# Graph stage of a four-layer graph network: logits built on ScalarE, shifted before the transpose, exponentiated on the way out of PSUM

## What is computed

```python
h = jnp.einsum('bnd,ade->bane', feat_in, W)
th = jnp.tanh(h)
attn_src = jnp.einsum('bane,aeo->bano', th, w_src)
attn_dst = jnp.einsum('bane,aeo->bano', th, w_dst)
attn = attn_src + jnp.swapaxes(attn_dst, 2, 3)
attn = jnp.where(attn >= 0, attn, LEAKY_ALPHA * attn)        # 0.2
attn = jnp.where(mask, jnp.float32(-999.0), attn)
attn = jax.nn.softmax(attn, axis=-1)
feat_out = jnp.einsum('banm,bame->bane', attn, h) + b
...
feat_out = jax.nn.elu(feat_out)
gate = jax.nn.sigmoid(feat_in @ H_w.T + H_b)
return gate * feat_out + (1.0 - gate) * feat_in
```

## Time and profile before

| | us |
|---|---|
| median of three runs | 2711.53 |
| the profiled execution | 2709.26 |
| its span | 2707.5 |
| busy in the span: TensorE, VectorE, ScalarE, GpSimd | 2640.9, 2417.2, 2346.9, 1804.9 |

### The profile page before, as it was taken

One profiled execution on the slowest core, in us unless ns is written; L12 is line 12 of the kernel. 1 busy time (PEld: TensorE's weight loads), 2 busy tenths in 40 slices (PEclk: granted clock), 3 DMA queues, 4 the chain that ended last, 5 costly groups with the idle time before them and its releaser, 6 DMA issues. The chain is left out here.

```text
span 2707.5 us, 66704 instructions
## 1 busy us (share of the span) xinstructions
PE 2640.9 (98%) x20128; PEld 2385.9 (88%) x20128; DVE 2417.2 (89%) x7209; ACT 2346.9 (87%) x6600; POOL 1804.9 (67%) x1550
## 2 busy tenths in 40 slices
PE   8999999999998999999999999999999999999996
PEld 7888888888887999999999999899999999999995
DVE  6998998898887999999999999899999999999995
ACT  7999999999998888888888888888888888888884
POOL 3777766766765677766666677766666666667665
PEclk9999999999999999999999999999999999999998
DMA  3011111111104888887778888878778887878775
GB/s 99 28 38 40 33 34 39 33 33 39 37 29 130 256 260 259 263 253 252 247 252 255 256 262 264 252 255 251 253 242 259 256 250 254 253 245 257 250 249 176
DMA packets 386754, 500.42 MB, mean 185 GB/s; under 512 B 58464, under 2 KB 349152, under 8 KB 386272
## 3 DMA queue, kind: packets, MB, share of 16 engines
q1 hardware_dynamic: 386400, 496.16, 58.2%
HBM read 219.24 MB, written 201.33 MB: 155 GB/s over the span
## 5 line engine op out<-in xcount | busy, mean ns | idle before, releaser
L794 ACT ACTIVATE probs<-logits,nmax 128x256 f32<-128x256 f32 x1152 | 571.8, 500 | 104.5 <-DVE turned_sb L1072 99.6
L570 POOL TENSOR_TENSOR probs<-probs,recs 128x1024 f32<-128x1024 f32 x288 | 545.9, 1896 | 107.8 <-DVE recs L1064 107.6
L1072 DVE STREAM_TRANSPOSE turned_sb<-probs 128x512 f32<-128x512 f32 x576 | 610.7, 1103 | 4.0 <-POOL probs L570 4.0
L1051 DVE CUSTOM_DVE_ANT_0 logits<-s,mask 128x256 f32<-128x256 f32 x1152 | 430.8, 420 | 84.1 <-PE s L1456 81.4
L548 POOL TENSOR_TENSOR residual<-x,br 128x384 f32<-128x384 f32 x192 | 191.0, 1017 | 455.9 <-DVE mix L1083 455.8
L787 ACT ACTIVATE stack<-split 64x768 fp32r<-64x768 f32 x576 | 484.8, 842 | 3.4
L76 PE MATMUL pj<-xt_hi,w_lo 128*128 128x256 f32 x1728 | 481.9, 279 | 0.8 <-DVE xt_lo L1036 0.8
L78 PE MATMUL pj<-xt_hi,w_hi 128*128 128x256 f32 x1728 | 481.0, 278 | 0.0
L77 PE MATMUL pj<-xt_lo,w_hi 128*128 128x256 f32 x1728 | 480.8, 278 | 0.0
L665 ACT ACTIVATE g_exps<-g_v,g_nmax 128x256 f32<-128x256 f32 x768 | 385.3, 515 | 3.0 <-DVE g_nmax L961 0.7
L779 ACT ACTIVATE split<-pj,bc 128x256 fp32r<-128x256 f32 x576 | 239.6, 467 | 163.2 <-PE pj L78 107.3
(11 more groups left out here) (118 smaller groups left out, 7401.3 us busy)
## 6 DMA issues: line engine op xcount, KB each, us to landing
turned<-turned_sb SPq DMA_DIRECT2D x288, 512.0 KB, 5.0
pt_copy<-turned SPq DMA_DIRECT2D x288, 512.0 KB, 4.6
stack<-split SPq DMA_DIRECT2D x576, 128.0 KB, 4.4
y<-out SPq DMA_DIRECT2D x128, 384.0 KB, 5.2
x<-y SPq DMA_DIRECT2D x96, 384.0 KB, 3.1
x<-x SPq DMA_DIRECT2D x32, 384.0 KB, 3.0
adj<-adj SPq DMA_DIRECT2D x128, 64.0 KB, 3.1
w_whole<-att_w SPq DMA_DIRECT2D x24, 192.0 KB, 2.9
```

The costliest lines, as they stand in the source:

```text
L570: pool.tensor_tensor(probs[:, heads, :, :].rearrange("p h t n -> p (h t) n"), probs[:, heads, :, :].rearrange("p h t n -> p (h t) n"), rec ...
L794: last = act.activation(probs[:, (HEADS * u + h) % 4, t, :], logits[:, h % 2, t, :], ACT.Exp, scale=-1.0, bias=nmax[:, u, h, t:t + 1], acc ...
L1051: last = dve.tensor_tensor_reduce(out=logits[:, h % 2, t, :], in0=s_ps[h % 2][:, t, :], in1=mask[u][:, t, :], scale=-HEAD_DIM ** -0.5, sca ...
L1072: last = dve.transpose(turned_sb[b][:, :, :].rearrange("p k (z h q) -> p k z h q", z=NT, h=2 * NT)[:, :, kt], probs[:, 2 * b:2 * b + 2, :, ...
```

## The change

The graph stage is written anew; the attention stage's functions stay (its first samples' order within `crossing()` is rewritten, and one store moves). The pieces:

```diff
+            def g_high_x(half, u, t):        # ScalarE; was the copy in g_lo_of_step on VectorE
+                act.activation(xt_hi[:, :, t * P:(t + 1) * P], pj_ps[g_X_BANK[t]][:, 0:D]..., ACT.Identity).then_inc(g_xt_hi_done, 1)
...
-                act.activation(g_v_sb[:, h % 3], s_ps[h % 2][:, :, :], ACT.Relu, scale=-0.8).then_inc(g_lrelu, 1)
+            def g_leaky(half, u, h):
+                g_targets_ready(act, half, u, h)
+                for t in range(NT):
+                    last = act.activation(g_v_of(u, h)[:, t, :], g_targets[u][:, h, :], ACT.Prelu, scale=-1.0,
+                                          bias=g_source[u][:, t, h:h + 1], alpha=LEAKY)
...
-                for t in range(NT):
-                    last = act.activation(g_exps[:, h % 4, t, :], g_v_sb[:, h % 3, t, :], ACT.Exp, scale=-1.0,
-                                          bias=g_nmax[:, u, h, t:t + 1], accum_out=g_sums[:, u, h, t:t + 1])
+                act.activation(g_pt_sb[:, g_pt_slot(u, h)], pt_ps[h % 2][:, :, :], ACT.Exp, scale=-1.0).then_inc(g_exped, 1)
...
                     last = dve.tensor_tensor_reduce(
-                        out=g_v_sb[:, h % 3, t, :], in0=s_ps[h % 2][:, t, :], in1=g_v_sb[:, h % 3, t, :], scale=-1.0,
+                        out=v[:, t, :], in0=s_ps[0][:, t, :], in1=v[:, t, :], scale=-1.0,
...
+            def g_subtract(half, u, h):      # VectorE, even heads
+                for t in range(NT):
+                    last = dve.scalar_tensor_tensor(v[:, t, :], v[:, t, :], g_nmax[:, u, h, t:t + 1], s_ps[0][:, t, :], ALU.subtract, ALU.max)
...
+            def g_subtract(half, u, h):      # GpSimd, odd heads
+                pool.tensor_tensor(v, v, g_nmax[:, u, h, :].unsqueeze(2).to_broadcast([P, NT, N]), ALU.subtract).then_inc(g_odd_shifted, 1)
...
-                pe.matmul(s_ps[h % 2][:, :, :], g_ident_r[:, :], g_mask[u][:, :, :], start=True, stop=False)
-                for t in range(NT):
-                    last = pe.matmul(s_ps[h % 2][:, t, :], g_z_left[u][:, t * P:(t + 1) * P], g_z_right[u][:, h, :], start=False, stop=t == NT - 1)
+                pe.matmul(s_ps[0][:, :, :], g_ident_r[:, :], g_mask[u][:, :, :], start=True, stop=True).then_inc(g_mask_laid, 1)
...
+                        pe.matmul(s_ps[1][i * GAT_DIM:(i + 1) * GAT_DIM, 0, :], ones, g_pt_sb[:, g_pt_slot(u, g * g_QUAD + i), kt, :], ...
...
+                    last = pe.matmul(pj_ps[g_SD_BANK][:, 0:N], g_sd[:, c, :], g_tt[:, c, :], start=c == 0, stop=c == DC - 1)
...
+                sp.dma_start(targets_dram[u], g_rows[g_TARGETS, :]).then_inc(g_rows_laid, 16)
+                sp.dma_start(g_targets[u][:, heads, :], targets_dram[u, heads, :]....partition_broadcast(P)...).then_inc(g_targets_spread[u][i], 16)
```

More of the change, by code:

```diff
@@ L19 @@
 GAT_HEADS, GAT_DIM = 12, 32
+LEAKY = 0.2
 HEADS, HEAD_DIM = 6, 64
@@ L41, in f32, with g_every_slot, sample @@
     return ap.bitcast(F32)
[L44 to L50, removed]
+def g_every_slot(slot):
+    def sample(k):
+        return divmod(k, 2) if 0 <= k < B else None
+    for k in range(B):
+        slot(sample(k + 1), sample(k), sample(k - 1), sample(k - 2), sample(k - 3), sample(k - 4))
 def every_slot_of_all_layers(slot, behind=3):
@@ new lines, in g_gate_tanh, with g_slot @@
+                act.activation(g_gate[u][:, t, :], pj_ps[g_GATE_BANK[t]][:, 0:D], ACT.Tanh, scale=0.5).then_inc(g_gate_done, 1)
+            def g_slot(far, nxt, cur, prev, old, done):
+                if prev:
+                    g_exp(*prev, 7)
+                    g_leaky(*prev, 11)
+                if old:
+                    g_elu_exp(*old)
+                if nxt and nxt != first:
+                    g_high_x(*nxt, 0)
+                if prev:
+                    g_exp(*prev, 8)
+                    g_copy_ct(*prev, 1)
+                    g_exp(*prev, 9)
+                if cur:
+                    g_leaky(*cur, 0)
+                    g_leaky(*cur, 1)
+                    g_gate_tanh(*cur, 0)
+                if prev:
+                    g_exp(*prev, 10)
+                if cur:
@@ L1268, in g_make_back @@
-            def g_make_back(half, u, t, cur, nxt):
+                pe.matmul(out, g_ones[:, :], g_hb[:, :], start=False, stop=True).then_inc(g_gate_made, 1)
+            def g_make_back(half, u, t):
+                if half == HALVES - 1:
+                    if (half, u, t) == (*g_even, 0):
+                        pe.wait_ge(g_gate_done, at(NT, *g_odd, NT))
+                    pe.wait_ge(g_back_read, at(NT, half, u, t))
+                elif t == 0:
+                    pe.wait_ge(g_tt_ready, at(NT, half, u, 2 * NT + 1))
+                else:
+                    pe.wait_ge(g_tt_ready, at(NT, half, u, 3 * NT))
@@ L1269, in g_make_back @@
                 if t == 0:
                     pe.wait_ge(g_ctx_read, at(g_GROUPS, half, u, g_GROUPS))
[L1271 to L1276 removed]
+                    pe.wait_ge(g_sums_read, at(1, half, u, 1))
@@ L1301, in g_four_contexts, with g_sums_of_four @@
+            def g_sums_of_four(u, g):
+                ones = g_sel[:, 1 + g * GAT_DIM:1 + (g + 1) * GAT_DIM]
+                for kt in range(NT):
+                    for i in range(g_QUAD):
+                        pe.matmul(s_ps[1][i * GAT_DIM:(i + 1) * GAT_DIM, 0, :], ones, g_pt_sb[:, g_pt_slot(u, g * g_QUAD + i), kt, :],
+                                         start=g == 0 and kt == 0, stop=g == g_GROUPS - 1 and kt == NT - 1)
             def g_four_contexts(half, u, g):
                 first = g * g_QUAD
-                pe.wait_ge(g_pt_even_read, g_evictions(half, u, first + g_QUAD - 2))
```

923 lines of the change are left out of this document (456 added, 467 removed).

## The result

| | before | changed |
|---|---|---|
| median | 2711.7 | 2643.6 |
| lowest and highest of 4 | 2705.3 to 2715.6 | 2642.3 to 2644.8 |
| profiled execution | 2709.26 | 2642.26 |
| its span | 2707.5 | 2640.5 |

The ratio is 0.9751, with a 95% interval of 0.9731 to 0.9771: 68 us faster. 2640 was predicted, within 2602 to 2685.

The account below looks back on a forecast made before the run. The bound was to move from ScalarE and TensorE to TensorE alone at 22.2 us, period 22.8. From 2709.3, minus 75 for 31 periods, plus 5 for the ends, gives 2639, stated as 2640 us, range 2602 to 2685.

Parts of the forecast that it names:

- The four sums: Graph stage, busy us per sample of each engine after the change: TensorE 22.2, VectorE 21.1, ScalarE 20.8, GpSimd 17.96.
- the leaky step: ScalarE's new leaky half, from one start to the next: taken as 0.40 us, within 0.36 to 0.50.
- the sources and targets: TensorE's three added full-width fp32 matmuls: at most 0.5 us each, taken as 1.5 us a sample.
- The period: Graph stage, time per sample: 22.8 us, 2.42 less than before, times 31 periods 75 us saved.
- the ends: First leaky half waits for two landings, +4 us; last sample drags four more heads into the crossing, +1.
- The bound: Graph stage: moves from ScalarE and TensorE at 24.9 and 24.7 us to TensorE alone at 22.2.
- three handoffs: TensorE's waits behind the state's turning and the exponentials of heads 3 and 7: 0.1 us each added.
- The sign named for it: Profile of the graph stage: TensorE's busy share highest, ScalarE and VectorE near 21 us a sample.
- The hold: VectorE standing behind GpSimd, up to 1.04 us each; one leaves TensorE the bound, two give 2661, three 2695; chance 0.15.
- The late transfer: Next sample's first spreading transfer on SP's list: 10.4 us until its leaky half needs it, landing 4.6 or 15.7.
- The rival of 2805: Spreading transfer lands in 15.7 us, too late for the leaky half; period 28.1, about 2805 us; chance 0.05.
- The copy of x: x's high part moved from VectorE to ScalarE: two copies, 0.8 us a sample added on ScalarE.

## Why the prediction was right, and where it was not

**The four sums.** ScalarE 20.8 predicted, 21.2 measured, with the leaky step at 0.40 as taken; what the other 0.4 is was not sought. VectorE 21.1 predicted, 21.6 measured: of this, 0.72 is the held gate product, so the list itself is 20.9. TensorE 22.2 predicted, 22.3 measured, or 22.0 without what a wait adds to the last matmul ahead of it. The sums at 0.89 instead of 1.00 a group and the sources and targets at 1.33 instead of 1.5 take off 0.5. A term that was put at nothing gives 0.3 back: with the scores matmuls gone, the groups of nine matmuls of 384 columns stand behind transposes or contexts in all four places, and their first one steps 0.26 to 0.28 (302.94, 305.82, 310.23 and 319.76); before, it stepped 0.17 in three places, behind scores matmuls, and 0.27 in the fourth, behind transposes. Together that is the 22.0. GpSimd 17.96 predicted, 18.7 measured, since one subtraction in each sample takes 1.69 in place of 1.04.

**The period.** 22.8 predicted, 22.89 measured, 31 times 2.33 is 72. The runs gained 68, the profiled executions 67, which leaves the +5 that was taken for the ends. The size held; that it did so with the bound named wrong is in part luck, as the next paragraph shows.

**The bound.** That the bound moves "to TensorE alone at 22.2" failed. TensorE's 0.60 of waiting matched the 0.65 allowed for (0.35 kept from before and 0.3 for three handoffs), but only 0.20 of it was a place named, the turning of the state. The contexts after heads 3 and 7 cost TensorE nothing that shows. The other 0.43 was the low part of x, which came late because VectorE was late. The step that failed is the comparison of busy sums alone: waits were added to TensorE's sum and none to VectorE's. VectorE has 1.30 of them, 0.49 behind the sums turned back and 0.57 behind leaky halves among them. (That 21.6 + 1.3 is as much as 22.3 + 0.6 proves nothing, since busy and idle time add up to the period on every engine.) The experiments show it both ways, 1.6 us off TensorE for nothing and 0.4 off VectorE for about 10 us. That TensorE's figure of 22.8 came out right was luck: it followed VectorE, and with VectorE out of the way the same matmuls went at 22.23 and, without the last wait, 22.08. The sign named for it, TensorE's busy share the highest, came true at 97.4% and could not tell.

**The hold.** The place was named (L986 against head 11's subtraction) and one hold was priced at up to 1.04 and called harmless. It was 0.72, and not harmless: taking it away at the price of a later head 11 gained 9 us, and halving it by an order that also hands TensorE its operand earlier gained 21. The forecast that VectorE's subtractions would stay out of the conflict because their second tensor is in PSUM held, and is worth more than the whole change: 97 us are lost with the other operand.

**The late transfer.** 10.4 us of room were estimated, 8.1 are there, and 5.5 are used. The rival of 2805 needed a landing of 15.7 us, scaled by size from one that was seen at the start; the same bytes landed in 5.5, so that scaling was wrong. Ahead of need there are 2.6 us and more, and a transfer issued 3.9 us ahead of its use costs 27 us.

**The copy of x.** Costed at 0.8 on ScalarE for a little more off VectorE's list; the trade is +22 us before and -21 us in the changed kernel.

## What to carry to other kernels

A busy share does not tell which engine sets the pace: one at 94% with a few short waits did here, and one at 97% followed it. Busy time plus idle time does not tell either, since it is the period for every engine. To learn which it is, take a microsecond from each in turn, and when forecasting, give every engine near the largest sum its waits, not the largest alone. And when work moves between engines, ask which pairs of instructions will then run side by side on VectorE and GpSimd, and where their operands lie; whether a second operand is read from PSUM or SBUF was worth 97 us here, and the change as a whole 68.

## What was not expected of the hardware

A VectorE instruction with one SBUF input and a scalar per partition, 128x256, steps 0.26 when GpSimd is still, and is held as well: its mean of 662 ns is above the 468 of the slower form with a PSUM input. In the same two kernels the minimum with zero, 128x768 with one input, reached 1.36 us against a median of 0.55, which it never did in the changed kernel (0.604 at most). Holds go in both directions: GpSimd's subtraction, 1.04 alone, had a mean of 1.24 with the mask from SBUF and 1.15 in the changed kernel.
